# Turning the order of the steps behind the last attention tile of a fused attention and expert kernel

## What is computed

```python
x = x + tanh(g_xattn[0]) * attention(layernorm(x), ctx_1024, ctx_1024, mask, Wq, bq, Wk, bk, Wv, bv, Wo, bo)
x = x + tanh(g_ffn[0]) * experts(layernorm(x), W1, b1, W2, b2, Wr, br)

def experts(x, W1, b1, W2, b2, Wr, br):          # cut
    logits = x @ Wr + br
    idx = argmax(logits)
    gates = softmax(logits)[idx]
    for ei in range(8):
        h = gelu(x @ W1[ei] + b1[ei], approximate=False)   # 128 -> 512
        out = out + (h @ W2[ei] + b2[ei]) * gates * (idx == ei)
```

## Time and profile before

| | |
|---|---|
| median of 3 runs | 282.6 us (280.78 to 283.52) |
| profiled execution | 282.11 us, of it 280.2 us from the first to the last instruction |
| mean granted TensorE clock | 0.989 |
| PE busy with matmuls | 231.7 us (83%) |
| DVE busy | 191.5 us (68%) |
| POOL busy | 182.0 us (65%) |
| ACT busy | 166.5 us (59%) |

### The profile page before, as it was taken

The page is one execution under the profiler, slowest core; times in us unless marked ns, Lnnn a source line. Parts: engine busy times, 40 slices in busy tenths (PEclk is TensorE's granted clock), DMA queues, the critical chain, the costliest instruction groups (busy, mean ns, idle before and its releaser), DMA issues.

```text
span 280.2 us, 10498 instructions
## 1 busy us (share of the span) xinstructions
PE 231.7 (83%) x3529; PEld 201.9 (72%) x3529; DVE 191.5 (68%) x639; ACT 166.5 (59%) x482; POOL 182.0 (65%) x222
## 2 busy tenths in 40 slices
PE   1357888989799888788988897797869999999992
PEld 1235677878678777567767676676769899999992
DVE  5535867888989889998678977777477434434431
ACT  1235678878778788566877775626464444444440
POOL 7374765757758889548988677740777377555464
PEclk9999999999999999999999999979999999999997
DMA  7811355627464573513425122133123443210010
GB/s 215 245 23 30 94 149 150 170 34 207 107 148 112 118 202 71 145 21 78 117 47 144 43 46 48 34 91 98 56 81 111 116 121 97 69 57 28 28 33 19
DMA packets 58535, 26.63 MB, mean 95 GB/s; under 512 B 38608, under 2 KB 53989, under 8 KB 58484
## 3 DMA queue, kind: packets, MB, share of 16 engines
q1 hardware_dynamic: 55204, 20.15, 29.4%
q0 software_dynamic: 2272, 4.46, 4.7%
q10 hardware_dynamic: 1008, 1.35, 1.7%
HBM read 16.70 MB, written 5.51 MB: 79 GB/s over the span
## 4 chain that ended last, share of the span: by engine, by line
PE 43%; DVE 18%; POOL 12%; issue 11%; DMA 6%; SPq 5%; ACT 4%; POOLq 1%; DVEq 0%
PE ps L751 12%; PE ps L794 5%; DMA kbd<-kT 4%; SPq L407 4%; PE ps L809 3%; DVE mx L1233 3%; PE ps L732 3%; PE ps L734 2%; PE ps L733 2%; PE ps L784 2%; PE ps L770 2%; POOL rows L513 2%; PE ps L836 2%; POOL rot L546 2%; POOL rot L540 2%
## 5 line engine op out<-in xcount | busy, mean ns | idle before, releaser
L563 POOL DMA_INDIRECT out<-fin,got x39 | 37.9, 972 | 28.1 <-DVE fin L1291 14.5
L1233 DVE TENSOR_REDUCE mx<-ps 128x16 f16<-128x1024 f32 x32 | 39.1, 1222 | 15.0 <-PE ps L809 14.8
L751 PE MATMUL ps<-w_f,hT 128*128 x312 | 44.6, 287 | 0.0
L513 POOL DMA_INDIRECT rows<-x_all,dest_i x32 | 33.3, 1040 | 17.2 <-DVE x_all L1068 9.7
L794 PE MATMUL ps<-vx,pr 128*64 128x32 f32 x1024 | 36.2, 224 | 4.4 <-DVE on L1168 2.4
L794 PEld LDWEIGHTS ps<-vx,pr 128*64 128x64 f32 x1024 | 32.7, 138 | 8.1 <-issue 2.9
L751 PEld LDWEIGHTS ps<-w_f,hT 128*128 128x128 f32 x312 | 37.8, 191 | 0.8
L593 ACT ACTIVATE pr<-ps 128x1024 f32<-128x1024 f32 x32 | 32.7, 1023 | 9.0 <-PE ps L836 8.6
L1291 DVE SCALAR_TENSOR_TENSOR fin<-ps,got 128x128 f32<-128x128 f32 x39 | 13.7, 351 | 35.5 <-PE ps L751 33.0
L540 POOL TENSOR_TENSOR rot<-qk,cf 128x256 f32<-128x256 f32 x32 | 23.4, 732 | 22.0 <-ACT qk L615 15.3
L527 POOL TENSOR_TENSOR stk<-rot,stk 128x256 f16<-128x256 f32 x32 | 21.5, 672 | 22.9 <-DVE stk L1245 22.9
(11 more groups left out here) (158 smaller groups left out, 584.7 us busy)
## 6 DMA issues: line engine op xcount, KB each, us to landing
kbd<-kT SPq DMA_DIRECT2D x128, 32.0 KB
got<-rows SPq DMA_DIRECT2D x39, 72.0 KB, 1.9
w_f<-in_W_rows SPq DMA_DIRECT2D x8, 256.0 KB, 2.9
w_r<-in_W_last_row SPq DMA_DIRECT2D x8, 256.0 KB, 3.3
w_f<-in_L_ffn_W SPq DMA_DIRECT2D x8, 256.0 KB, 5.0
x_all<-in_x SPq DMA_DIRECT2D x3, 512.0 KB, 4.5
xt_all<-in_x_t SPq DMA_DIRECT2D x3, 512.0 KB, 4.8
ct_all<-in_ctx SPq DMA_DIRECT2D x3, 512.0 KB, 4.2
```

Source lines behind the costliest of these rows:

```text
L513: pool.indirect_dma_start(out=rows, out_offset=bass.IndirectOffsetOnAxis(ap=dest_i[:, t:t + 1], axis=0), in_=x_all[:, t, :], in_offset=Non ...
L563: pool.indirect_dma_start(out=out_d, out_offset=bass.IndirectOffsetOnAxis(ap=got_i[:, u % GOT, R_ID:R_ID + 1], axis=0), in_=fin[:, u % FRI ...
L751: mm = pe.matmul(o, hT[:, par, c, :], w2_f[:, bass.ds(e, 1), c, :].rearrange("p o n -> p (o n)"), start=False, stop=(c == FC - 1))
L1233: dve.tensor_reduce(mx[:, t % 2, 0:H], ps_s[:, :].rearrange("p (h k) -> p h k", k=S), AX.X, ALU.max).then_inc(mx_done, 1)
```

## The change

In steps from 34 on the order within the engines changes, and some tables with it.

- PE: the score stack (last tile: step 34) comes first, then the weighted values, then the turned output, then the turning of the expert tile and the first layer. Before: weighted values, turning, first layer, turned output, score stack.
- DVE: normalising the attention output, the sum with x and its statistics come ahead of the expert tile's `z` and rest; in step 35 group 3's places do too. For group 4 the sum, reciprocal and gate come ahead of the places, and the copies of the row counts (`end_i`, `end_f`) behind them.
- ACT: the exponential of group 4 moves from step 39, ahead of that step's Gelu, to the end of step 38, between two small activations on a tile of two columns (Exp, then Gelu) that bring the table loads about.
- POOL: the power of group 4 moves ahead of the scatters of step 37; group 3's last four scatters all stand in step 37; outputs 0 to 2 move behind the last row scatters (steps 43 and 44 in place of 39 and 40), and later outputs two places forward or back against the drains (output u at step 38 + u in place of 40 + u).
- Banks: second-layer results go round banks 5, 0 and 1; the turned tile uses bank 7 from u = 3.

```diff
         def t_bank(u):
-            return 6 if u < 4 else 6 + u % 2
+            return 6 if u < 3 else 6 + u % 2
         def y_bank(u):
-            return 5 if u < 4 else (5, 0)[u % 2]
+            return (5, 0, 1)[u % 3]
         def out_step(u):
-            return F0 + 5 + u // 2 if u < 3 else min(max(SCATTER_AT) - 2 + u, STEPS - 1)
+            return min(max(max(SCATTER_AT) + 1 + u // 2, F0 + 4 + u), STEPS - 1)
-        SCATTER_AT = {..., 32: 4, 36: 3, 37: 2, 38: 2, 41: 3, 42: 2}
+        SCATTER_AT = {..., 32: 4, 36: 3, 37: 4, 41: 3, 42: 2}
...
         POOL, step(i)
+                if i == max(GROUP_AT):
+                    rstd2_of(GROUP_AT[i])
                 for _ in range(SCATTER_AT.get(i, 0)):
                     scatter()
...
         ACT, step(i)
-                if i - 2 in GROUP_AT:
+                if i - 2 in GROUP_AT and i - 2 < max(GROUP_AT):
...
                     act.activation(hT[:, u % 2, :, :].rearrange("p c n -> p (c n)"), bank[2 + u % 2], ACT.Gelu,
                                    scale=1.0 / W_SCALE).then_inc(f_gelu, 1)
+                if i == max(GROUP_AT) + 1:
+                    act.activation(warm[:, 1, :], gates[:, :], ACT.Exp)
+                    gate_exponential(GROUP_AT[i - 1])
+                    act.activation(warm[:, 2, :], gates[:, :], ACT.Gelu)
...
         PE, step(i): weighted_values, score_stack, normalised_turned are the old statements as functions
+                if i < F0:
+                    weighted_values(i)
+                else:
+                    score_stack(i)
+                    weighted_values(i)
+                    normalised_turned(i)
+                    if tile(i - F0):
+                        rows_transposed(i - F0)
+                    if tile(i - F0 - 1):
+                        first_layer(i - F0 - 1)
...
         DVE, step(i): expert_rows, normalised, sum_with_x, sum_stats likewise
+                normalised(i)
+                if i >= F0:
+                    sum_with_x(i)
+                    sum_stats(i)
+                    if i == F0 + 1 and third is not None:
+                        route_place(third)
+                    expert_rows(i)
...
+                if third is not None and i > T + 6:
+                    route_sum(third)
+                    route_recip(third)
+                    route_gates(third)
+                if third is not None and i != F0 + 1:
                     route_place(third)
...
                     route_dest(third)
+                if third is not None and i > T + 6:
+                    route_ends(third)
```

More of the change, by code:

```diff
@@ L346, in build @@
         RSTD_AT = {1: 1, 3: 2, 7: 3, 11: 4, 15: 5, 19: 6, 23: 7}
-        SCATTER_AT = {**{i: 1 for i in (*range(15, 21), *range(22, 32))}, 32: 4, 36: 3, 37: 2, 38: 2, 41: 3, 42: 2}
+        SCATTER_AT = {**{i: 1 for i in (*range(15, 21), *range(22, 32))}, 32: 4, 36: 3, 37: 4, 41: 3, 42: 2}
         DRAIN_AT = (46, 58, 70)
@@ L548, in step @@
                     rstd_of(RSTD_AT[i])
-                if i in GROUP_AT:
+                if i in GROUP_AT and i < max(GROUP_AT):
                     rstd2_of(GROUP_AT[i])
@@ L595, in step @@
                 if t == T - 1:
-                    act.activation(warm[:, :], gates[:, :], ACT.Gelu)
+                    act.activation(warm[:, 0, :], gates[:, :], ACT.Gelu)
                 t = i - 3
@@ L1143, in tiles_begun, with expert_rows @@
                 then(dve.tensor_scalar(first[:, N1:NS], cf[0:1, C_IOTA:C_IOTA + N2], done[0:1, 0:1], float(P), ALU.add, ALU.mult))
-            def step(i):
-                before, after, third = (GROUP_AT.get(i - n) for n in (1, 2, 3))
+            def expert_rows(i):
                 u = i - F0
@@ L1170, in step, with sum_with_x, sum_stats @@
                                       ALU.mult).then_inc(on_done, 1)
+            def sum_with_x(i):
+                t = i - 6
+                if live(t):
+                    dve.wait_ge(op_done, t + 1)
+                    dve.wait_ge(lx_ev, t + 1)
+                    dve.tensor_tensor(x_all[:, t, 0:QX], ps_op, x_all[:, t, 0:QX], ALU.add).then_inc(x2_done, 1)
+            def sum_stats(i):
+                t = i - 6
+                if live(t):
+                    dve.wait_ge(x2_done, t + 1)
+                    dve.bn_stats(st6b[:, t % 2, :], x_all[:, t, 0:D]).then_inc(bn2_s, 1)
+                    dve.wait_ge(bn2_s, t + 1)
+                    dve.bn_aggr(x_all[:, t, R_MEAN:R_MEAN + 2], st6b[:, t % 2, :]).then_inc(bn2_a, 1)
+                if i in GROUP_AT:
+                    route_var(GROUP_AT[i])
+            def step(i):
+                before, after, third = (GROUP_AT.get(i - n) for n in (1, 2, 3))
+                normalised(i)
[5 more added lines that the diff above has]
+                    expert_rows(i)
                 t = i
@@ L1207, in step @@
                     route_cand(after)
+                if third is not None and i <= T + 6:
+                    route_sum(third)
                 if third is not None:
-                    route_sum(third)
                     route_dest(third)
+                if third is not None and i > T + 6:
+                    route_ends(third)
                 for t in STATS_AT.get(i, ()):
@@ L1216, in step @@
                     route_first(after)
-                if third is not None:
+                if third is not None and i <= T + 6:
                     route_recip(third)
```

83 lines of the change are left out of this document (57 added, 26 removed).

## The result

| | before | changed |
|---|---|---|
| median of 20 runs of each | 281.28 us | 283.83 us |
| range of the runs | 279.70 to 283.52 | 281.64 to 286.13 |
| ratio, 95% interval | | 1.009 (1.0066 to 1.0115) |
| profiled execution | 282.11 us, span 280.2 | 283.38 us, span 281.6 |
| PE busy / DVE / ACT / POOL | 231.7 / 191.5 / 166.5 / 182.0 us | 234.8 / 191.0 / 167.2 / 183.1 us |

The kernel became 0.9% slower, 2.55 us in the medians and 1.27 us in the two profiled executions. I therefore measure from the end of the last copy of the maxima (`mxT`, tile 31, the last common event ahead of the change: 190.28 us before, 189.95 after) and call this **the distance**.

What follows compares the result with a forecast made beforehand. PE's unbroken train of expert tiles sets the end, with tile 13's late loads as second limit. Delays outweighing gains made +1.1 us: 282.11 to 283.2 profiled, plus 0.5 for the median, 283.7; 8 in 10 range 280.5 to 285.0.

Steps and rivals of the forecast that it cites:

- my bounds: For the whole change: +0.4 us if first layers behind waits are quicker, +1.5 if landings are slower; chance 0.50.
- my 1.1: Total forecast: the kernel 1.1 us slower, profiled execution from 282.11 to 283.2 us.
- Step 34: Score stack and weighted values ahead of turning tile 0: the last `pr` starts 0.7 us later, at 193.4 us.
- Steps 35 and 36: DVE's sums ahead of `z` and rest, turned output waiting uncovered: variance of group 4 0.9 us later, at 200.65 us.
- POOL's power: Group 4's power behind only three scatters: starts at 200.9 instead of 201.61 us, scaled router values 0.7 us sooner.
- Banks: Three banks for second layers: `fin` waits of 1.61 and 1.06 us go, the first spent in full on steps 34 to 37.
- The exponential: Step 38's exchange puts tile 5's hi copy behind two table loads: DVE's sum for group 4 1.1 us later, at 208.7.
- The second limit, the late loads: Tile 13's loads follow group 4's scatters: they start at 219.7 against 218.61 us, its `z` at 222.8 against 221.68.
- Both limits say the same: Second layer 5 leaving 1.0 us later and tile 13's late loads both put the loss at +1.1 us.
- The clock, my slower rival: PE's clock falls to half speed on new idle gaps, 1.5 us per fall: 285.2 us with one; chance 0.07.

Runs made afterwards that it cites:

- orders back: Changed kernel with the old order within PE's and DVE's steps, banks, exponential, POOL's queue and outputs as changed; distance 83.79 us, ratio to before 1.001.
- exponential back: Changed kernel with group 4's exponential in step 39 again, ahead of Gelu 4, without the two small activations; distance 87.09 us, ratio to before 1.006.
- changed again: The changed kernel once more with nothing altered, to see the spread; distance 88.62 us, ratio to before 1.006.
- PE's order back: Changed kernel with the old order in PE's steps, DVE's order still the new one; distance 87.99 us, ratio to before 1.012.
- two banks back: Changed kernel with the expert sums in two banks as before the change; distance 87.27 us, ratio to before 1.008.
- drains back: Changed kernel with POOL's drains before outputs 6, 18 and 30 as before the change; distance 87.06 us, ratio to before 1.010.

## Why the prediction was right, and where its steps were off

The sign and the median (283.7 forecast, 283.83 measured) held. The size did not: +1.27 us between the profiled executions lies in my bounds (+0.4 to +1.5), but +1.72 by distance and +2.55 between the medians lie beyond them. The hit on the median is luck: the kernel before measured 281.28 over 20 runs, 1.32 less than the 282.6 that I started from, and the loss is 1.45 more than my 1.1, and the two errors cancel.

**Step 34.** `pr` was to start 0.7 us later behind the hi copy of tile 0; it is 3.07 against 2.32 of distance, 0.75. Right, and undoing PE's order brings it back (2.33).

**Steps 35 and 36.** The mechanism was right, the size too small. I had the variance 0.9 us late; it is 1.96. Two things are missing in my sum. First layer 0 took 0.95 us too (195.69 to 196.64), not the 0.67 I used, and began 0.34 us behind the turning of tile 1, where it was 0.16 before. And the turning of tile 2 itself waited for the rest of tile 1 (done at 198.51): it started at 198.65, and first layer 1 only 0.32 us behind it (198.97), where it is 0.11 in the train; I had that layer 0.1 us behind the rest. Together this is some 0.8 us of the 1.06. First layer 2 adds more: I had second layer 2 at 204.2, by distance 13.92 and level with the kernel before (14.00); it came at 15.44. These 1.5 us are what the sum lacks at the train's start, too, where I forecast 1.0 us and the profile shows 2.58. A held-up PE is slow in starting its next expert weights: first layers 0, 1, 2, 5 and 6 were, and I had counted three of the five. That the weights' register addresses are the reason stays my reading. That DVE's order is the harmful half, and not PE's, is shown by undoing each: -2.43 us by the first, no gain by the second (+1.22, a fall of the clock included).

**POOL's power.** Forecast 0.7 us sooner; it came 0.38 later by distance (12.95 against 12.57). This is the step that failed in sign: the queue was freed as worked out, POOL was idle for 1.34 us, but the variance that it waits for was another us later. With the orders back it is 1.45 sooner, so only the size of the previous step was wrong.

**Banks.** Both waits for `fin` went, as forecast, and the train still left later. Put on the kernel before alone they are worth 1.15 us at second layer 5 (from `pr` on); put on the new order half a us at most. The 2.67 us of waits were not to be had in full: in the changed kernel 0.49 us of wait stand before the turning of tile 3 instead, for its `z`, and first layer 2 behind it is slow.

**The exponential.** "DVE's sum 1.1 us later": it was 2.50 later by distance (19.77 against 17.27). From second layer 2 to the sum are 4.33 us, against 3.27 in the kernel before and 3.28 with the exponential back, so 1.05 us belong to the exchange, as forecast, and the other 1.44 are the delay with which second layer 2 itself comes. DVE's idle of 2.20 us for the hi copy stood where I put it in the order, and about 1 us later in time. Where the Trainium skill ("ScalarE: Activation LUTs", section "What ACT_TABLE_LOAD costs") gives a drain of some 1.38 us for each switch, the new rows again have none: from the first load at 206.17 to the hi copy at 209.22 are 3.05 us, two loads of 1.28, one exponential and two small activations.

**The second limit, the late loads.** Half wrong. They moved by 1.83 us of distance (30.16 against 28.33), but the train moved by 2.58, so `z` of tile 13 waited for nothing. Part of this is chance: the last row scatter moved by 2.50 (26.86 against 24.36), and the first load followed its start by 3.30 us instead of 3.97. What stood there before, the late tile 13, came off the loss again. PE's second layers before and after it takes up the second set of expert numbers (step 47), kernel before and changed kernel:

```profile
220.97 0.23 PE L749 MATMUL ps<-b_h,ch 128*128 128x128 f16 x1
224.76 0.23 PE L749 MATMUL ps<-b_h,ch 128*128 128x128 f16 x1 [0.99 <-ACT hT L663]
```

```profile
223.25 0.22 PE L758 MATMUL ps<-b_h,ch 128*128 128x128 f16 x1
226.06 0.23 PE L758 MATMUL ps<-b_h,ch 128*128 128x128 f16 x1 [0.85 <-ACT hT L668]
```

3.79 us from one second layer to the next before, 2.81 after: 0.98 us given back, which covers the 2.58 - 1.72 = 0.86. In the second profile of the changed kernel, where the load is late, nothing is given back. "Both limits say the same" was a coincidence of two wrong sizes.

**The clock, my slower rival, at 0.07.** A fall was given too small a chance and too high a price. In the stretch 190 to 216 us the clock fell in four of six profiles with DVE's new order (changed again, PE's order back, exponential back, two banks back) and in none of eight without it. But I priced a fall at 1.5 us, and by second layer 2 or 5 it cost 0.66 us (changed again), 0.55 (exponential back) and 0.25 (two banks back). The section "HAM oscillation — how this bites in real kernels" of the page "TensorE: Matmul & The Clock Gate" in the Trainium skill, which I cited against new waits, agrees with these rows only in part: the falls do stand behind idle gaps of PE, but the gaps it speaks of are long ones, and here none was over 1.5 us. Why the medians are 2.55 us apart and the first profiles only 1.3 stays open: a fall (0.25 to 0.7 us), tile 13's load coming late again (1.2 in changed again) and a long third drain (0.15 to 0.8) can each lengthen an execution, and the other timed runs have no profile.

## What to carry to other kernels

When stages of two pipelines overlap on in-order engines, "the old pipeline's work first" is no rule: DVE's `z` and rest had all they needed, and putting them behind a sum that had to come back from PE made two engines wait for each other in turn; put what is ready ahead of what is waited for. Before moving a table exchange or another block of some us, list what is queued behind it and route around it: here the waiting engine had 1.1 us of work that needed only what the exchange had already made. And measure from the last event that two kernels share: runs of one kernel lay over 1% apart, and two profiles of the kernel before agreed to 0.04 us in that distance. It is no cure for all: two profiles of the changed kernel differ by 1.85 us, so look for a fall of the clock and for late loads before you compare.

## What the runs showed of the hardware that I had not expected

The place of the last common event varied between 188.1 and 194.3 us in kernels that are the same up to there; with the clock at 1.00 from 180 to 190 us it was 188.1 to 191.9, with a fall in that stretch 190.0 to 194.3. In the four profiles with a fall to 1.2 GHz behind 190 us, waits of PE of 0.2 to 1.5 us, none longer, stood ahead of it; but the first profile of the changed kernel and the one with the drains back have nearly the same waits and stay at 1.00, and so does the kernel before with waits of 1.61 and 1.06 us. POOL's gap at a drain took from 2.6 to 4.7 us with the same kind of DMAs in flight. The first late load followed the start of the last row scatter by 2.65 to 4.34 us over the fourteen profiles, which is enough to bring tile 13's wait or take it away.
